# Attention over 1,601 keys: a smaller first piece ahead of the loop, swapped keys read across quadrants, key parts written by ScalarE

## The chip, the cores and the metric

The kernel runs on one core of one Trainium2 chip. The metric is device time in microseconds of one execution. Three runs of the kernel before gave 707.81, 712.16 and 712.87 us; the median is 712.16 us. The execution that was profiled took 710.4 us, of which 707.4 us lie between its first and last instruction.

## What is computed

`x` has 4 batches of 256 rows of 128, `ctx_1024` 4 batches of 1,601 rows of 128. All is float32, with 16 heads of 8.

```python
x = x + L0_xattn(layernorm(x), ctx)       # layernorm again on both sides, rotary turn of q and k, a bias by distance, gate
x = x + tanh(layernorm(x) @ W1 @ W2 @ W3 + b)
x = x + L1_xattn(layernorm(x), ctx, ctx)  # plain projections with biases, mask, softmax, output projection
x = x + experts(layernorm(x))             # two of 8 experts by a gate
```

The rotary turn of layer 0 is `k * cos + swapped(k) * sin`, where `swapped` exchanges the halves of each head. Scores must be exact to float32, so a key or query is stored as three bfloat16 parts (high, middle, low) whose products are summed in one matmul.

## The kernel before

The context is cut into 13 tiles of 124 keys, and four groups of 4 heads go over each tile. That gives 52 units per batch and layer, and 416 in all: units 0 to 207 are layer 0 (batches 0 to 3), the others layer 1. TensorE (PE) runs one written-out loop over pairs of units: `scores` of the next two units (matmuls L369 for the bias, L375 for q times k), then `beside` (side work by a table of slots), then `values` of this pair (L390), then `beside` again. A slot is the number of the unit within its batch. ScalarE (ACT) turns each unit's scores into `probs` by one Exp (L811). PSUM banks 0 to 3 hold scores, 4 and 5 the sums, and two side banks, LOW (6) and HIGH (7), all side work. A side bank is filled again only when what was in it has been read (`seen`).

The keys and values of layer 0 are made chunk by chunk, as side work of the batch before: `keys_at` gives the slots. `CHUNKS` is 4, 3, 3 and 3 tiles. For each chunk PE makes the turned and the swapped key product (L314, two banks, with weights `w0c[:, 2]` and `w0c[:, 3]`), the layer 1 key product (L317) and the values (L323). VectorE (DVE) multiplies by the tables (L950, L955), adds the two (L959), casts high parts (L965, L976) and middle parts (L1000, L1002), adds the layer 1 bias (L974) and writes the values (L992, L994). GpSimd (POOL) makes the rests and the low parts (L740 to L746). SyncE (SP) issues the DMAs that place six copies of the parts in `k_side` (L609) and store them for layer 1 (L610 to L616).

SP works its list strictly in the order written, and a wait holds all behind it. At the start it loads all of `x`, all tokens of batch 0 (L582, L583) and then the weights (L661); ACT's list loads the tables, the constant rows of `k_side` and `q_side` and the bias. Ahead of the loop come the norm and the queries of all of `x`, and chunk 0 of batch 0. A small sample of scores then gives each row's shift (`sample`, `make_shift` L1028, DMA L648), on which the scores of unit 0 wait. The same shift gates every batch: `scores` of a batch's unit 0 waits for `shift_in`. A batch's row scales go from `turn_rstd` (L305) through DRAM (L594, L600) to `norm_context` on POOL (L730), which the batch's chunk 0 needs.

The mask is checked in 16 pieces, loaded from POOL's queue (L723) and reduced on DVE (L1014), all beside layer 0.

## Time and profile before

| | |
|---|---|
| median of three runs | 712.16 us |
| profiled execution | 710.4 us, span 707.4 us |
| PE busy | 576.8 us (82%) |
| ACT busy | 408.8 us (58%) |
| DVE busy | 269.7 us (38%) |
| POOL busy | 119.3 us (17%) |
| first Exp of the loop | at 89.3 us |
| batches 0 to 3 of layer 0 (first Exp to first Exp) | 114.2, 88.7, 79.7, 61.8 us |
| batches 0 to 3 of layer 1 | 55.6, 60.7, 59.2, 57.0 us |
| from the last unit to the end | about 41 us |

Busy shares are means over stages that have different limits. So the stages are read one by one: which engine works all the time, and what ends the waits of PE and ACT.

### The profile page before, as it was taken

What the parts mean: (1) busy time and instruction counts of PE and PEld (TensorE: products, weight loads), DVE (VectorE), ACT (ScalarE), POOL (GpSimd) and SP (SyncE); (2) the same over time, 40 slices, a digit from 0 to 9 for tenths busy, and PEclk for the clock granted to TensorE, in tenths of its full rate; (3) what the DMA queues carried; (4) which work ended last, traced back from release to release, by engine and by line L of the source; (5) the groups of instructions that cost most, each with busy time, mean ns of one, the idle gap of its engine ahead of it and who ended that gap; (6) DMA issues with size and microseconds to landing.
All of it is one profiled execution on the core that took longest, in us unless ns stands there. A gap on an engine that the chain in (4) does not pass through costs nothing.

```text
span 707.4 us, 15097 instructions
## 1 busy us (share of the span) xinstructions
PE 576.8 (82%) x6349; PEld 284.5 (40%) x6349; DVE 269.7 (38%) x703; ACT 408.8 (58%) x437; POOL 119.3 (17%) x132
## 2 busy tenths in 40 slices
PE   4046199589759889989999999999989998999744
PEld 2033045335334445544554544443443443353231
DVE  0036246246615662266525112320540443243243
ACT  1001055336435465754777789899859878988600
POOL 1043123343414340054200100000000000000000
PEclk9998579789969999999999999999999999999955
DMA  9542417749472766017718103602700720000000
GB/s 234 119 143 68 130 33 196 223 120 247 127 231 70 178 167 224 23 38 192 204 56 184 63 3 68 151 2 48 171 9 1 158 66 5 2 2 9 2 0 11
DMA packets 55496, 70.37 MB, mean 99 GB/s; under 512 B 5684, under 2 KB 47680, under 8 KB 55360
## 3 DMA queue, kind: packets, MB, share of 16 engines
q1 hardware_dynamic: 52576, 57.82, 30.7%
q0 software_dynamic: 1280, 6.56, 3.9%
q10 hardware_dynamic: 1568, 4.99, 3.0%
q8 instruction: 51, 0.84, 0.5%
q14 instruction: 21, 0.17, 0.1%
HBM read 37.45 MB, written 18.84 MB: 80 GB/s over the span
## 4 chain that ended last, share of the span: by engine, by line
PE 58%; issue 11%; DVE 9%; DMA 8%; ACT 7%; SPq 3%; POOL 2%; POOLq 0%; ACTq 0%; DVEq 0%
PE ps L390 20%; PE ps L375 11%; PE ps L369 7%; ACT probs L811 6%; DMA ctx_tokens<-in_ctx 5%; PE ps L323 4%; PE ps L314 3%; PE ps L317 2%; PE ps L503 2%; SPq L609 1%; DVE y L1194 1%; PE ps L437 1%; DMA r_scratch<-rstd_turned 1%; PE ps L424 1%; PE ps L430 1%
## 5 line engine op out<-in xcount | busy, mean ns | idle before, releaser
L811 ACT ACTIVATE probs<-ps 124x1024 f32<-124x1024 f32 (+1 forms) x416 | 399.8, 1022 | 200.2 <-PE ps L375 198.1
L390 PE MATMUL ps<-probs,values 124*9 124x256 f32 (+1 forms) x3328 | 223.3, 387 | 0.4 <-DVE out_sums L1035 0.4
L375 PE MATMUL ps<-q_side,k_side 63*124 63x256 bf16 (+1 forms) x1664 | 164.2, 283 | 11.6 <-ACT probs L811 9.8
L375 PEld LDWEIGHTS ps<-q_side,k_side 63*124 63x124 bf16 (+1 forms) x1664 | 98.6, 133 | 86.1 <-ACT probs L811 55.6
L390 PEld LDWEIGHTS ps<-probs,values 124*9 124x9 f32 (+1 forms) x3328 | 71.3, 90 | 100.2 <-issue 43.5
L369 PE MATMUL ps<-bias_g,bias_w 64*124 64x512 bf16 (+1 forms) x416 | 87.2, 415 | 14.7 <-DMA q_side<-shift 14.1
L753 POOL TENSOR_TENSOR post_rstd<-post_rstd,power 128x2 f32<-128x2 f32 x12 | 8.4, 697 | 319.6 <-DVE post_rstd L1083 319.6
L369 PEld LDWEIGHTS ps<-bias_g,bias_w 64*124 64x124 bf16 (+1 forms) x416 | 28.2, 132 | 56.8 <-issue 36.9
L1035 DVE COPY out_sums<-ps 128x512 f32<-128x512 f32 x16 | 11.0, 690 | 94.2 <-PE ps L390 94.2
L314 PE MATMUL ps<-ctx_normed,w_centred 128*128 128x372 f32 (+2 forms) x64 | 28.5, 572 | 7.1 <-POOL ctx_normed L730 6.6
L1021 DVE TENSOR_REDUCE sample_max<-ps 128x8 f32<-128x512 f32 x32 | 20.6, 686 | 32.2 <-PE ps L340 32.2
L323 PE MATMUL ps<-w_values,ctx_turned 128*124 128x256 f32 (+1 forms) x104 | 32.1, 426 | 0.0
L1194 DVE SCALAR_TENSOR_TENSOR y<-ps,comb,y 128x128 f32<-128x128 f32 x64 | 22.5, 351 | 15.8 <-PE ps L503 13.9
L740 POOL TENSOR_TENSOR k<-k,k_parts 128x372 f32<-128x372 f32 (+2 forms) x16 | 15.0, 937 | 71.7 <-DVE k_parts L965 71.7
L317 PE MATMUL ps<-ctx_turned,wk_sb 128*128 128x372 f32 (+2 forms) x32 | 16.6, 604 | 10.2 <-DVE k L950 10.2
L845 ACT ACTIVATE w_centred<-ps 128x512 f32<-128x512 f32 x1 | 0.6, 597 | 41.8 <-PE ps L267 41.8
L261 PE MATMUL ps<-gamma_beta,w 128*128 128x1 f32 x8 | 1.9, 354 | 26.3 <-DMA wvg_sb<-in_wvg 26.3
L992 DVE TENSOR_TENSOR values<-ps,rstd 124x256 f32<-124x256 f32 (+2 forms) x32 | 12.0, 375 | 29.2 <-PE ps L323 29.2
L323 PEld LDWEIGHTS ps<-w_values,ctx_turned 128*124 128x124 f32 (+1 forms) x104 | 18.1, 196 | 12.1 <-issue 10.0
L744 POOL TENSOR_TENSOR k_parts<-k,k_parts 128x372 bf16<-128x372 f32 (+2 forms) x16 | 16.0, 1001 | 39.5 <-DVE k_parts L1000 39.5
L925 DVE BATCH_NORM_STATS2 row_stats<-ctx_tokens 124x6 f32<-124x128 f32 (+1 forms) x52 | 11.3, 279 | 29.0 <-DMA ctx_tokens<-in_ctx 29.0
L950 DVE SCALAR_TENSOR_TENSOR k<-ps,beta_products,k_cos_sb 128x372 f32<-128x372 f32 (+2 forms) x16 | 10.1, 633 | 26.7 <-PE ps L314 26.5
(177 smaller groups left out, 485.9 us busy)
## 6 DMA issues: line engine op xcount, KB each, us to landing
k_side<-k_scratch SPq DMA_DIRECT2D x24, 400.2 KB, 8.8
k_side<-k_parts SPq DMA_DIRECT2D x48, 93.0 KB, 3.9
k_scratch<-k_parts SPq DMA_DIRECT2D x16, 279.0 KB, 4.2
v_scratch<-values SPq DMA_DIRECT2D x4, 936.0 KB, 6.2
values<-v_scratch SPq DMA_DIRECT2D x4, 936.0 KB, 14.1
mask_q<-in_mask POOLq DMA_DIRECT2D x8, 400.5 KB, 5.0
ctx_turned<-in_ctx_t SPq DMA_DIRECT2D x4, 800.5 KB, 7.0
ctx_normed<-r_scratch SPq DMA_DIRECT2D x4, 800.5 KB, 4.1
```

The source lines that it names most:

```text
L314: pe.matmul(ps[:, bank, 0:w], w0c[:, i, :], cn[:, k_0:k_1], start=True, stop=True).then_inc(made[bank], 1)
L317: pe.matmul(ps[:, LOW, 0:w], wk1[:], ct[:, k_0:k_1], start=True, stop=True).then_inc(made[LOW], 1)
L323: last = pe.matmul(ps[0:r, bank, 2 * D * i:2 * D * i + 2 * D], ct[:, TS * t:TS * t + r], wvv[:].rearrange("p l d -> p (l d)"), start=True, ...
L369: pe.matmul(ps[0:width, bank, :], G["bias_w"][rows, at], G["bias_g"][rows, t:t + 1, :].broadcast_to((HALF, 2, SQ)), start=True, stop=False ...
L375: last = pe.matmul(ps[0:width, bank, SQ * i:SQ * (i + 1)], kst[rows, j % 2, 2 * g + i, at], qst[rows, j % 2, 2 * g + i, :], start=not bias ...
L390: last = pe.matmul(ps[32 * i:32 * i + VC, ACC + g // 2, SQ * (g % 2):SQ * (g % 2) + SQ], v[0:rows, j % 2, t, h, :], p[0:rows, u % 4, SQ * ...
L503: pe.matmul(ps[:, bank, :], xn[:, b * SQ + 128 * t:b * SQ + 128 * t + 128], ew[:, 4 * i:4 * i + 4, :].rearrange("p e d -> p (e d)"), start ...
L740: pool.tensor_tensor(ka[:, s, 0:w], ka[:, s, 0:w], kp0[:, s, 0, 0:w], ALU.subtract).then_inc(rest0, 1)
L744: pool.tensor_tensor(kp0[:, s, 2, 0:w], ka[:, s, 0:w], kp0[:, s, 1, 0:w], ALU.subtract).then_inc(lo0, 1)
L811: act.activation(p[0:rows, u % 4, :], ps[0:rows, s:s + 2, :].rearrange("p a n -> p (a n)"), ACT.Exp)\
L1021: dve.tensor_reduce(mx[:, c, H8 * half_:H8 * half_ + H8], ps[:, bank, :].rearrange("p (h k) -> p h k", k=SAMPLE), AX.X, ALU.max).then_inc( ...
L1194: add = dve.scalar_tensor_tensor(out=out[:, t, :], in0=ps[:, bank, D * i:D * i + D], scalar=comb[:, t, e:e + 1], in1=out[:, t, :], op0=ALU ...
```

## The change

The chunks become 1, 4, 4 and 4 tiles. Only the first 256 rows of `x` are normed and projected ahead of the loop, and chunks 0 and 1 (5 tiles) of batch 0; the other queries, and the centred `x`, are made in slots 11, 13, 17 and 19 of batch 0. The row statistics of `x` come from a second copy of it with rows on the partitions (`x_tok`), by the same instructions as those of the tokens. The row scales of batch 0 are spread by matmuls (L290 of the kernel after) and no longer go through DRAM. SP's order of loads is new and now also carries the tables, the constant rows and the bias; ACT's list carries the weights. `store_keys` is split in `place_keys` and `store_keys`.

The swapped key product is gone: DVE reads the one product in four pieces of 32 partitions, each from 32 partitions away, against a sine table that is rearranged. The sum of the two goes to POOL, the layer 1 bias and all high and middle parts to ACT, 3 to 9 units after the matmul. The mask check moves to the batches from 3 on (batch 3 of layer 0, and 0 to 2 of layer 1).

SP's queue from the tokens of batch 1 to the shift of batch 0, first before and then after the change (`lo0` counts low parts written, `q_lo` those of the queries, `bn_done` token statistics, `side6_read` readings of LOW):

```order
L582 DMA ctx_tokens<-in_ctx 124x12x128 [waits bn_done]
L583 DMA ctx_tokens<-in_ctx 113x128
L627 DMA q_side<-q_parts 16x8x256 [waits q_lo]
L627 DMA q_side<-q_parts 16x8x256 x5
L609 DMA k_side<-k_parts 16x8x496 [waits lo0]
L609 DMA k_side<-k_parts 16x8x496 x5
L610 DMA k_scratch<-k_parts 384x1x496
L612 DMA v_scratch<-v 128x576 [waits side6_read]
L614 DMA k_scratch<-k_parts 384x1x496 [waits lo1]
L648 DMA q_side<-shift 1x8x256 [waits side6_read]
L648 DMA q_side<-shift 1x8x256
```

```order
L646 DMA k_side<-k_parts 16x8x124 [waits lo0]
L646 DMA k_side<-k_parts 16x8x124 x5
L669 DMA q_side<-q_parts 16x8x256 [waits q_lo]
L669 DMA q_side<-q_parts 16x8x256 x5
L646 DMA k_side<-k_parts 16x8x496 [waits lo0]
L646 DMA k_side<-k_parts 16x8x496 x5
L614 DMA ctx_tokens<-in_ctx 124x128 [waits bn_done]
L614 DMA ctx_tokens<-in_ctx 124x4x128 [waits bn_done] x2
L614 DMA ctx_tokens<-in_ctx 124x3x128 [waits bn_done]
L617 DMA ctx_tokens<-in_ctx 113x128
L690 DMA q_side<-shift 1x8x256 [waits side6_read,gaps_in0]
L690 DMA q_side<-shift 1x8x256
```

The tokens of batch 1 were ahead of the queries and the keys and now stand between the keys and the shift; the stores of keys and values now follow the shift.

DVE's work on one chunk of keys (chunk 1 of batch 1), before and after (`side6_filled` and `side7_filled` count fillings of LOW and HIGH):

```order
L950 SCALAR_TENSOR_TENSOR k<-ps,beta_products,k_cos_sb 128x372 [waits side6_filled,lo0]
L955 SCALAR_TENSOR_TENSOR k_swapped<-ps,beta_products,k_sin_sb 128x372 [waits k0_full,side7_filled]
L959 TENSOR_TENSOR k<-k,k_swapped 128x372 [waits side7_read,side6_read]
L965 CAST k_parts<-k 128x372 [waits k0_full,k0_out1,k_in3]
L974 TENSOR_SCALAR k<-ps,columns_sb 128x372 [waits side6_filled,k1_out1,lo1]
L976 CAST k_parts<-k 128x372 [waits side6_read]
L992 TENSOR_TENSOR values<-ps,rstd 124x32x8 [waits side7_filled,v1_out1]
L994 COPY v<-ps 124x32x8
L992 TENSOR_TENSOR values<-ps,rstd 124x16x8 [waits side6_filled]
L994 COPY v<-ps 124x16x8
L1000 CAST k_parts<-k 128x372 [waits rest0]
L1002 CAST k_parts<-k 128x372 [waits rest1]
```

```order
L1119 SCALAR_TENSOR_TENSOR k<-ps,beta_products,k_cos_sb 128x496 [waits side6_filled,lo0,table_in0]
L1126 SCALAR_TENSOR_TENSOR k_swapped<-ps,beta_products,k_sin_sb 32x496 [waits k0_full]
L1126 SCALAR_TENSOR_TENSOR k_swapped<-ps,beta_products,k_sin_sb 32x496 x3
L1153 TENSOR_TENSOR values<-ps,rstd 124x32x8 [waits side6_filled,v1_out1]
L1155 COPY v<-ps 124x32x8
L1153 TENSOR_TENSOR values<-ps,rstd 124x32x8 [waits side7_filled]
L1155 COPY v<-ps 124x32x8
```

Twelve instructions for 3 tiles became nine for 4; all five table products read LOW, which stays taken until the last.

ACT's list behind the first units of batch 0 held Exps alone until the gate of batch 1; now it reads:

```order
L889 ACTIVATE probs<-ps 124x1024 [waits scores_ready] x4
L915 ACTIVATE k<-ps,columns_sb 128x496 [waits side7_filled,k1_out0,lo1]
L916 ACTIVATE k_parts<-ps,columns_sb 128x496
L889 ACTIVATE probs<-ps 124x1024 [waits probs_used,scores_ready] x3
L932 ACTIVATE k_parts<-k 128x496 [waits k0_full,k0_out0,k_in0]
L889 ACTIVATE probs<-ps 124x1024 [waits probs_used,scores_ready]
L922 ACTIVATE k_parts<-k 128x496 [waits rest1]
L889 ACTIVATE probs<-ps 124x1024 [waits probs_used,scores_ready] x2
L938 ACTIVATE k_parts<-k 128x496 [waits rest0]
```

Five key instructions per chunk stand between the Exps, three of them behind POOL (`k0_full`, `rest1`, `rest0`).

The diff, cut to its core:

```diff
-CHUNKS = [(0, 4), (4, 7), (7, 10), (10, KT)]
+CHUNKS = [(0, 1), (1, 5), (5, 9), (9, KT)]
...
+KEY_STEPS = [1 + (t1 - t0 + 1) // 2 for t0, t1 in CHUNKS]
...
-        first = {0: (0, 1), 6: (0, 2), 12: (0, 3), 23: (1, 0), 29: (1, 1), 36: (1, 2), 43: (1, 3)}
+        first = {0: (0, 2), 6: (0, 3), 23: (1, 0), 26: (1, 1), 33: (1, 2), 40: (1, 3)}
     elif j < NB - 1:
-        first = {6 + 6 * n: (j + 1, n) for n in range(NC)}
+        first = {at: (j + 1, n) for n, at in enumerate((6, 9, 16, 23))}
     else:
         return None
     for at, (b, n) in first.items():
-        if slot - at in (0, 2, 3, 4):
-            return b, n, (0, 2, 3, 4).index(slot - at)
+        if slot - at in (0, 2, 3)[:KEY_STEPS[n]]:
+            return b, n, (0, 2, 3).index(slot - at)
...
-                    for bank, i in ((LOW, 2), (HIGH, 3)):
-                        fill(bank, "k0", b, n)
-                        pe.matmul(ps[:, bank, 0:w], w0c[:, i, :], cn[:, k_0:k_1], start=True, stop=True).then_inc(made[bank], 1)
-                elif k == 1:
-                    fill(LOW, "k1", b, n)
-                    pe.matmul(ps[:, LOW, 0:w], wk1[:], ct[:, k_0:k_1], start=True, stop=True).then_inc(made[LOW], 1)
+                    fill(LOW, "k0", b, n)
+                    pe.matmul(ps[:, LOW, 0:w], w0c[:, 2, :], cn[:, k_0:k_1], start=True, stop=True).then_inc(made[LOW], 1)
+                    fill(HIGH, "k1", b, n)
+                    pe.matmul(ps[:, HIGH, 0:w], wk1[:], ct[:, k_0:k_1], start=True, stop=True).then_inc(made[HIGH], 1)
                 else:
-                    bank, tiles = ((HIGH, range(t0, t0 + 2)), (LOW, range(t0 + 2, t1)))[k - 2]
+                    bank, tiles = (LOW, HIGH)[k - 1], range(t0 + 2 * (k - 1), min(t0 + 2 * k, t1))
                     fill(bank, "v", b, n)
...
-            x_means()
-            x_variances()
             beta_products()
+            centre_weights()
             pe.wait_ge(ident_in, 16)
-            turn_rstd(0)
-            pe.wait_ge(both_pow, 1)
-            for last in spread_x(rb, (4, 5)):
-                last.then_inc(spread, 1)
-            centre_weights()
-            pe.wait_ge(seen[LOW], side.of(LOW, "weights"))
+            pe.wait_ge(rs_ready, 1)
+            spread_rstd(4, 0).then_inc(r_spread, 1)
+            pe.wait_ge(x_pow, 1)
+            spread_x(3, 0, range(2), 1).then_inc(spread, 1)
             first_queries()
-            pe.wait_ge(seen[HIGH], side.of(HIGH, "weights"))
-            pe.wait_ge(cols_in, 48)
-            for k in range(4):
+            pe.wait_ge(wk1_in, 32)
+            for k in range(KEY_STEPS[0]):
                 keys(0, 0, k)
-            pe.wait_ge(gaps_in, 64)
+            pe.wait_ge(rs_ready, 2)
+            spread_rstd(5, 1).then_inc(r_spread, 1)
+            for k in range(KEY_STEPS[1]):
+                keys(0, 1, k)
+            pe.wait_ge(gaps_in[0], 64)
             for c in range(2):
                 sample(0, c)
             turn_maxima(0)
+            pe.wait_ge(rs_ready, 3)
+            for n, bank in ((2, LOW), (3, HIGH)):
+                fill(bank, "r", n)
+                spread_rstd(bank, n).then_inc(made[bank], 1)
+            pe.wait_ge(x_pow, 2)
+            pe.wait_ge(cn_ready, 2)
+            spread_x(4, 0, range(2, 6), 1).then_inc(spread, 1)
+            spread_x(5, 0, range(6, XT), 1).then_inc(spread, 1)
+            pe.wait_ge(const_in, 48)
+            pe.wait_ge(qa_scaled, 2)
+            for u in range(2):
+                scores(u)
             pe.wait_ge(zeroed, 1)
+            pe.wait_ge(xq_ready, 2)
...
+            load_tokens(0, 0)
+            sp.dma_start(xtok[:, 0:2, :], G["x_tok"][:, 0:2, :]).then_inc(xtok_in, 16)
+            load_tokens(0, 1)
+            sp.dma_start(x[:, 0:SQ], G["x_t"][:, 0:SQ]).then_inc(x_in, 16)
+            load_turned_chunk(0, 0)
+            load_turned_chunk(0, 1)
+            load_tables(0)
+            load_tokens(0, 2)
+            load_tokens(0, 3)
+            sp.dma_start(xtok[:, 2:XT, :], G["x_tok"][:, 2:XT, :]).then_inc(xtok_rest_in, 16)
+            sp.dma_start(x[:, SQ:NT], G["x_t"][:, SQ:NT]).then_inc(xrest_in, 16)
+            for n in (2, 3):
...
+            load_tables(1)
+            for r in (HD - 2, HD - 1):
+                sp.dma_start(kst[r::HD, 0].rearrange("p h k -> p (h k)"), G["ones_row"].broadcast_to((H, H8 * SKP))).then_inc(gaps_in[0], 16)
+                sp.dma_start(qst[r::HD].rearrange("p s h n -> p (s h n)"), G["zero_row"].broadcast_to((H, 2 * H8 * SQ))).then_inc(gaps_in[0], 16)
+            for dst, src in ((G["bias_w"], "bias_k"), (G["bias_g"], "bias_q"), (G["pick"], "pick_in")):
+                sp.dma_start(dst[:], G[src]).then_inc(const_in, 16)
+            place_keys(0, 0)
             load_queries_of(0)
+            place_keys(0, 1)
+            for n in range(NC):
+                load_tokens(1, n)
+            sp.wait_ge(gaps_in[0], 64)
+            load_shift(0)
             store_keys(0, 0)
-            load_shift(0)
+            store_keys(0, 1)
+            for r in (HD - 2, HD - 1):
+                sp.dma_start(kst[r::HD, 1].rearrange("p h k -> p (h k)"), G["ones_row"].broadcast_to((H, H8 * SKP))).then_inc(gaps_in[1], 16)
+            for n in (2, 3):
+                place_keys(0, n)
+                store_keys(0, n)
             for n in late:
                 if n != "columns":
                     sp.dma_start(late[n][:], G[n]).then_inc(late_in, 16)
-            for n in range(1, NC):
-                store_keys(0, n)
             load_turned(1)
...
+                pool.wait_ge(seen[HIGH], side.of(HIGH, "k1", b, n))
+                pool.tensor_tensor(k1[:, s, 0:w], k1[:, s, 0:w], kp1[:, s, 0, 0:w], ALU.subtract).then_inc(rest1, 1)
+                pool.wait_ge(seen[LOW], side.of(LOW, "k0", b, n))
+                pool.tensor_tensor(ka[:, s, 0:w], ka[:, s, 0:w], kb[:, 0:w], ALU.add).then_inc(k0_full, 1)
                 pool.wait_ge(hi0, c + 1)
                 pool.tensor_tensor(ka[:, s, 0:w], ka[:, s, 0:w], kp0[:, s, 0, 0:w], ALU.subtract).then_inc(rest0, 1)
-                pool.wait_ge(hi1, c + 1)
-                pool.tensor_tensor(k1[:, s, 0:w], k1[:, s, 0:w], kp1[:, s, 0, 0:w], ALU.subtract).then_inc(rest1, 1)
+                pool.wait_ge(mid1, c + 1)
+                pool.tensor_tensor(kp1[:, s, 2, 0:w], k1[:, s, 0:w], kp1[:, s, 1, 0:w], ALU.subtract).then_inc(lo1, 1)
                 pool.wait_ge(mid0, c + 1)
                 pool.tensor_tensor(kp0[:, s, 2, 0:w], ka[:, s, 0:w], kp0[:, s, 1, 0:w], ALU.subtract).then_inc(lo0, 1)
-                pool.wait_ge(mid1, c + 1)
-                pool.tensor_tensor(kp1[:, s, 2, 0:w], k1[:, s, 0:w], kp1[:, s, 1, 0:w], ALU.subtract).then_inc(lo1, 1)
...
+            for j in range(NB - 1, NJ - 1):
+                first = 4 * (j - NB + 1)
+                look_at_mask(first)
+                look_at_mask(first + 1)
+                if j <= NB:
+                    for k in range(2):
+                        post_power(2 * (j - 1) + k)
+                    look_at_mask(first + 2)
+                    query_parts(j - 1)
+                else:
+                    post_power(2 * NB + j - NB - 1)
+                    look_at_mask(first + 2)
+                look_at_mask(first + 3)
+            post_power(3 * NB - 2)
+            post_power(3 * NB - 1)
...
+                for lag, part in ((9, middle_of_first), (7, middle_of_second), (6, high_of_first), (3, second_keys)):
+                    key = keys_at(j, i - lag)
+                    if key is not None and key[2] == 0:
+                        part(*key[:2])
...
-                dve.wait_ge(made[HIGH], side.of(HIGH, "k0", b, n))
+                                         op0=ALU.add, op1=ALU.mult)
                 if c:
                     dve.wait_ge(k0_full, c)
-                dve.scalar_tensor_tensor(out=kb[:, 0:w], in0=ps[:, HIGH, 0:w], scalar=beta_cols[:, 3:4], in1=k_sin[:, k_0:k_1],
-                                         op0=ALU.add, op1=ALU.mult).then_inc(seen[HIGH], 1)
-                dve.wait_ge(seen[LOW], side.of(LOW, "k0", b, n))
-                dve.wait_ge(seen[HIGH], side.of(HIGH, "k0", b, n))
-                dve.tensor_tensor(ka[:, s, 0:w], ka[:, s, 0:w], kb[:, 0:w], ALU.add).then_inc(k0_full, 1)
-                if c >= 2:
-                    b2, n2 = chunk_before(b, n, 2)
-                    dve.wait_ge(k_in[n2], QL * (b2 + 1))
-                    dve.wait_ge(k0_out[s], 16 * (c // 2))
-                dve.wait_ge(k0_full, c + 1)
-                dve.tensor_copy(kp0[:, s, 0, 0:w], ka[:, s, 0:w]).then_inc(hi0, 1)
-
-            def second_keys(b, n):
-                c, s = NC * b + n, n % 2
-                w = CHUNK_KEYS[n][1] - CHUNK_KEYS[n][0]
-                if c >= 2:
-                    dve.wait_ge(lo1, c - 1)
-                    dve.wait_ge(k1_out[s], 16 * (c // 2))
-                dve.wait_ge(made[LOW], side.of(LOW, "k1", b, n))
-                dve.tensor_scalar(k1[:, s, 0:w], ps[:, LOW, 0:w], col["bk"], None, ALU.add).then_inc(seen[LOW], 1)
-                dve.wait_ge(seen[LOW], side.of(LOW, "k1", b, n))
-                dve.tensor_copy(kp1[:, s, 0, 0:w], k1[:, s, 0:w]).then_inc(hi1, 1)
-
-            def both_values(b, n):
+
+                for to in range(0, 128, 32):
+                    at = to ^ 32
+                    last = dve.scalar_tensor_tensor(out=kb[to:to + 32, 0:w], in0=ps[at:at + 32, LOW, 0:w], scalar=beta_cols[at:at + 32, 2:3],
+                                                    in1=k_sin[at:at + 32, k_0:k_1], op0=ALU.add, op1=ALU.mult)
+                last.then_inc(seen[LOW], 1)
```

## Rows read from the trace of the kernel before

**Rows 1.** The page, the chain that ended last, by engine
```profile
PE 58%; issue 11%; DVE 9%; DMA 8%; ACT 7%; SPq 3%; POOL 2%; POOLq 0%; ACTq 0%; DVEq 0%
```

**Rows 2.** Busy us by stage: PE, PEld, DVE, ACT, POOL; then clock, DMA share, GB/s
```profile
0.00:38.00 38.00, 7.33 (x20) 4.67 (x20) 1.57 (x4) 2.43 (x3) 2.90 (x7) 1.00 0.74 177
89.30:203.50 114.20, 90.69 (x851) 45.67 (x849) 52.14 (x149) 50.41 (x52) 40.93 (x42) 0.86 0.60 172
203.50:292.20 88.70, 83.23 (x873) 42.70 (x871) 44.38 (x118) 51.13 (x54) 25.26 (x27) 0.95 0.50 140
292.20:372.00 79.80, 77.09 (x860) 39.56 (x858) 39.62 (x84) 51.15 (x55) 24.01 (x28) 1.00 0.42 113
305.00:345.00 40.00, 37.87 (x370) 19.10 (x364) 26.57 (x57) 21.32 (x22) 15.84 (x19) 1.00 0.56 146
```

**Rows 3.** Timeline of the start: start us, us, engine, line; idle before
```profile
1.64 30.94 SPq L583 DMA_DIRECT2D ctx_tokens<-in_ctx  x1
...
72.28 3.83 SPq L609 DMA_DIRECT2D k_side<-k_parts  x6
...
80.27 0.61 PE L340 MATMUL ps<-k_side,q_side 62*128 62x64 bf16 x16 [10.44 <-DMA k_side<-k_parts]
...
88.16 0.69 PE L369 MATMUL ps<-bias_g,bias_w 64*124 64x512 bf16 x2 [2.40 <-DMA q_side<-shift]
```

**Rows 4.** DMA packets in 53 to 62 us and in 124 to 139 us
```profile
DMA packets 1208, 0.62 MB, mean 69 GB/s; under 512 B 0, under 2 KB 1208, under 8 KB 1208
...
DMA packets 2204, 3.55 MB, mean 237 GB/s; under 512 B 218, under 2 KB 1882, under 8 KB 2202
```

**Rows 5.** Timeline, hand-over of row scales to batch 1
```profile
124.13 3.81 SPq L609 DMA_DIRECT2D k_side<-k_parts  x6
...
129.24 0.38 PE L305 MATMUL ps<-ident,rstd 124*13 124x124 f32 x1 [4.91 <-POOL rstd L734]
...
144.88 3.46 PE L314 MATMUL ps<-ctx_normed,w_centred 128*128 128x496 f32 x4 [6.07 <-POOL ctx_normed L730]
```

**Rows 6.** Timeline, hand-over of the shift to batch 1
```profile
190.15 3.83 SPq L609 DMA_DIRECT2D k_side<-k_parts  x6
...
202.40 0.69 PE L369 MATMUL ps<-bias_g,bias_w 64*124 64x512 bf16 x2 [11.73 <-DMA q_side<-shift]
```

**Rows 7.** Groups of the page: count, busy us, mean ns, idle before
```profile
L314 PE MATMUL ps<-ctx_normed,w_centred 128*128 128x372 f32 (+2 forms) x64 | 28.5, 572 | 7.1 <-POOL ctx_normed L730 6.6
```

**Rows 8.** The same by shape
```profile
L744 POOL TENSOR_TENSOR k_parts<-k,k_parts 128x496 bf16<-128x496 f32 x4 | 4.9, 1232 | 10.3 <-DVE k_parts L1000 10.3
...
L955 DVE SCALAR_TENSOR_TENSOR k_swapped<-ps,beta_products,k_sin_sb 128x496 f32<-128x496 f32 x4 | 2.9, 731 | 0.7 <-PE ps L314 0.6
...
L1014 DVE TENSOR_REDUCE checks<-mask_q 128x1 f32<-128x801 int32 x8 | 7.7, 968 | 0.0
...
L1028 DVE TENSOR_SCALAR shift<-ps 16x256 bf16<-16x256 f32 x8 | 3.3, 411 | 11.5 <-PE ps L350 11.5
...
L297 PE MATMUL ps<-out_sums,w_centred 128*128 128x512 f32 x8 | 3.7, 605 | 0.5 <-ACT w_centred L845 0.5
...
L851 ACT ACTIVATE q_parts<-att 128x512 bf16<-128x512 f32 x2 | 1.2, 622 | 4.3 <-DVE att L903 4.3
```

**Rows 9.** Timeline inside batch 2, PE and DVE
```profile
307.37 1.05 PE L390 MATMUL ps<-probs,values 124*9 124x256 f32 x16
...
308.35 1.13 PE L323 MATMUL ps<-w_values,ctx_turned 128*124 128x256 f32 x4
...
309.41 0.43 PE L369 MATMUL ps<-bias_g,bias_w 64*124 64x512 bf16 x2
...
310.43 1.13 PE L323 MATMUL ps<-w_values,ctx_turned 128*124 128x256 f32 x4
...
313.81 0.33 DVE L1044 TENSOR_SCALAR inside<-den 128x256 bf16<-128x256 f32 x1
...
318.48 0.60 DVE L950 SCALAR_TENSOR_TENSOR k<-ps,beta_products,k_cos_sb 128x372 f32<-128x372 f32 x1
...
318.99 0.60 DVE L955 SCALAR_TENSOR_TENSOR k_swapped<-ps,beta_products,k_sin_sb 128x372 f32<-128x372 f32 x1
...
319.13 0.89 PE L317 MATMUL ps<-ctx_turned,wk_sb 128*128 128x372 f32 x2 [2.13 <-DVE k L950]
```

**Rows 10.** Who waited for whom, PE: us in total, times, longest us
```profile
PE ps L305 <- POOL rstd L734: 10.8, 3, 4.9
```

675 lines of the change are left out of this document (395 added, 280 removed).

## The prediction

> **What bounds the kernel now.** I read the chain that ended last first: PE holds 58% of it [rows 1], so a stage counts by what PE waits for in it. The table by stage comes next [rows 2]. In the first 38 us PE is busy for 7.3 us and the DMA engines for 74%: this stage is bound by transfers. In batch 0 PE is busy 90.7 of 114.2 us, in batch 1 83.2 of 88.7, in batch 2 77.1 of 79.8, while ACT, with its 52 Exps, is busy about 51 us in each: layer 0 is bound by PE, plus PE's waits. In the timeline of the start the reader should see one issue on SP's queue that takes 30.9 us (the tokens of 512 B rows, beside ACT's large loads), keys placed from 72.3 us, the sample at 80.3 and the first scores at 88.2 [rows 3]. Last come two hand-overs where PE stands still: 4.9 and 6.1 us for the row scales [rows 5], 11.7 us for the shift [rows 6].
>
> **The start: -22.7 us.** The work ahead of the loop shrinks to 5 tiles and 256 rows, so arithmetic no longer sets its end; SP's queue does. Ahead of the first keys it now carries 1,601 token rows and 1,024 rows of `x`, 2,625 packets of 512 B, and 5.4 MB in larger ones; ACT's queue adds 0.9 MB. Packets of 512 B ran at 1,208 in 9 us, 134 per us [rows 4]: 20 us. The other 6.2 MB take 26 us at the 237 GB/s of a busy stretch [rows 4]. One after the other that is 46 us; wholly overlapped at 237 GB/s, 7.6 MB take 32. I take 40, starting at 1 us. Keys of chunk 0, queries and keys of chunk 1 follow: 3 + 5.7 (768 packets of 512 B) + 3.8 (as an issue of six, [rows 3]) = 12.5 us, to 53.5. The sample needs only the first two; from the sample to the first scores it was 88.2 - 80.3 = 7.9 us [rows 3], so by itself the shift could be there at about 57. But the tokens of batch 1 now stand between: 1,601 packets, 12 us. The shift lands at 65.5, and the first scores move from 88.2 to 65.5. Bounds: at the 177 GB/s of the first 38 us [rows 2], 9.7 MB take 55 us and with the tail the scores start at 80 (-8); if the large loads hide the small packets, at 52 (-36). What is late next is the shift, behind those tokens.
>
> **PE's work inside the loop: -9 us.** The turned and swapped products were 64 passes, 28.5 us [rows 7]; 60 lie inside the loop, half go: -13.3. One tile fewer of the other products: -0.8 (values of two tiles take 1.06 us, 308.35 to 309.41, [rows 9]). Added are the late queries and the centred `x`: a 512-column product takes 3.7 / 4 = 0.93 us [rows 8], five of these: +4.7. All of it is on the path.
>
> **LOW is held longer: +9.6 us.** DVE frees LOW after five instructions of 496 columns. One took 731 ns, and pieces of 32 partitions should cost no less: 16 partitions by 256 take 411 ns [rows 8], and nothing in the rows makes fewer partitions cheaper. DVE begins one before the last ends: 318.48 to 318.99 for one that lasts 0.60 [rows 9], so 4 x 0.66 + 0.73 = 3.4 us, 3.6 with both ends. PE wants LOW again after the layer 1 product (0.95), values (0.98, 307.37 to 308.35), scores (1.02, 309.41 to 310.43) [rows 9], near 3.0: it waits 0.6 us in nine chunks, +5.4. In batches 1 and 2 the second chunk comes three slots after the first, with the softmax finish (4.7 us, 313.81 to 318.48, [rows 9]) between them on DVE. PE waited 2.13 us there before [rows 9]. Now: finish 4.7 + table products 3.4, less the some 4 us that PE takes to come round, is 4.2; twice 2.1 more, +4.2. Below, if the pieces overlap better and finish fits: 0. Above: double, 19.
>
> **ACT's new work: 0 us.** 11 chunks x 5 instructions x 0.6 us (a 512-column one takes 622 ns, [rows 8]) = 33 us, 3 for the small chunks, 2 for queries: 38. The cover is ACT's idle time beside PE: in 40 us of batch 2 it was busy 21.3 [rows 2] and gets about 15 more. The writes fall 3, 6, 7 and 9 units after a chunk's product, mostly beside the next side work. If the cover were gone, all 38 would show.
>
> **POOL's sum, DVE's relief, no DRAM trip for batch 0's scales: 0.** POOL has 5 instructions of 1.1 to 1.23 us [rows 8] per chunk, 6 us in the 11 that a chunk's seven slots last; it was busy 25 of 89 us.
>
> **Hand-overs.** The scales of batch 1 now wait on POOL until the last parts of batch 0 are made (ACT writes a middle part after unit 15), then on SP behind the placing, the stores and 0.5 MB of late weights. Before, from the last placing at 124.1 to the first product it was 20.8 us [rows 5]; the mask load is gone (-0.4 MB), the late weights come (+4 us), PE arrives 8 slots and two centring steps later. I get 3 + 6.5 us of waiting against 4.9 + 6.1 before: 0, bounds -4 and +7. The shift of batch 1 took 12.2 us from the placing at 190.2 [rows 6]; now one more tile and the load of the next context (0.8 MB) are ahead, the mask is not: **+2** (0 to +8). Of the 10.8 us for the power [rows 10] the third wait goes, since POOL makes it one chunk earlier: **-2.7**.
>
> **The mask beside layer 1: +3.** 16 reductions of 0.97 us [rows 8] leave DVE beside batches 0 to 2, where DVE rarely ended PE's waits, and join a chain that PE follows closely; batch 3 had one there already. I take 1 us in each of three batches (0 to +12).
>
> **Sum:** -22.7 - 9 + 9.6 + 0 + 2 - 2.7 + 3 = -19.8, from the profiled 710.4 to 690.6. The median lies 1.8 above the profiled execution: **692 us**.
>
> **The rivals.**
> - *No overlap between the pieces.* The four change quadrant each time. If DVE starts each after the last has ended, it is 5 x 0.73 + 5 x 0.04 = 3.85 us, +0.45 in 11 chunks: **697 us**. For it: only instructions on the same partitions are seen overlapping [rows 9]. The Trainium skill, "VectorE: DVE Perf Modes", section "Two Vector instructions with no wait between them", has such a rule: an instruction whose input or output starts in another quadrant than the last one in that memory starts only when all earlier ones have finished. No run here shows such a piece; by that rule this rival is the forecast.
> - *A late queue.* The loads run at the pace of the first 38 us, and the tokens hold the shift until 78: start -10, **705 us**. For it: one issue was held for 30.9 us [rows 3].
> - *Nothing is late.* Start at 55 and half of LOW's waits: -10 - 5, **677 us**. Against it: the 12 us of tokens are plain in the order.
> - *ScalarE's line (slower).* ACT works in order, and three of five key writes wait for POOL, which waits for DVE. If POOL is late, the Exps behind stand, and PE's next scores with them, in each of 11 chunks. It decides from 20 of the 38 us on: then the gain is gone (**712**); with all, **730 us**. For it: after the finish in batches 1 and 2 DVE is late by 4 us. Against: ACT has 19 free us in 40 [rows 2].
>
> **How the numbers follow.** Forecast (684 to 696) 0.42; no overlap (694 to 702) 0.22; nothing late (675 to 684) 0.14; late queue (702 to 709) 0.11; ScalarE's line (709 to 730) 0.07; a hand-over that grows by more, anywhere, 0.04. The range 677 to 707 leaves out under 0.2. The three runs span 5 us, so about 1% is what a measurement tells from no change: faster means under 705. That is 0.42 + 0.22 + 0.14 + 0.05 = 0.83; within 1% 0.09; slower 0.08.
>
> **What would show it.** First Exp at 66 to 67 us, the DMA engines busy without a gap before it, and PE's wait there ended by the shift. In batches 1 and 2 PE waits for a DVE table product, 0.6 us a chunk and 4 at the second. Starts of the four pieces 0.65 us apart (or 0.75 and more: no overlap). ACT's idle time ended by scores, not by POOL; if `k0_full` or `rest0` ends many of its waits, the forecast is wrong on the slow side. The wait for the shift of batch 1 is 12 to 15 us. If the first Exp comes before 58 or after 74, the queue was misjudged.

## The result: 1.6% slower, and the profile after

The changed kernel took 721.47 us (median of four runs, 720.17 to 723.66) against 710.84 us before (four runs, 707.81 to 712.87). The ratio is 1.0156, with a 95% interval from 1.0105 to 1.0208. The forecast was 692 us with a range of 677 to 707: wrong in sign. The profiled execution took 723.66 us, its span is 721.9.

First Exp to first Exp of each batch, from the two timelines, in us:

| | start | 0 | 1 | 2 | 3 | 4 | 5 | 6 | 7 |
|---|---|---|---|---|---|---|---|---|---|
| before | 89.3 | 114.2 | 88.7 | 79.7 | 61.8 | 55.6 | 60.7 | 59.2 | 57.0 |
| after | 59.6 | 122.9 | 90.5 | 85.7 | 72.5 | 55.6 | 68.7 | 68.4 | 57.0 |
| difference | -29.7 | +8.7 | +1.8 | +6.0 | +10.7 | 0 | +8.0 | +9.2 | 0 |

The start gained even more than forecast. The loop of layer 0 gave 16.5 us of it back, and batches 3, 5 and 6, in which the only new work is the check of the mask, gave back 27.9. Batch 4 carries four pieces of the mask as well and did not change.

The page of the kernel after, the chain that ended last, by engine and by line (against [rows 1]):

```profile
PE 50%; DVE 13%; issue 12%; ACT 8%; DMA 8%; SPq 6%; POOL 2%; POOLq 0%; DVEq 0%; ACTq 0%
PE ps L411 18%; PE ps L395 9%; ACT probs L889 7%; PE ps L389 7%; DVE k_swapped L1126 5%; DMA mask_q<-in_mask 4%; PE ps L341 4%; PE ps L333 2%; DVE y L1348 2%; SPq L646 2%; PE ps L524 1%; DMA ctx_tokens<-in_ctx 1%; DVE k L1119 1%; DMA q_side<-shift 1%; DVE den L1203 1%
```

PE's share fell from 58 to 50% and DVE's rose from 9 to 13. Two names are new on the chain, the four pieces of the swapped product (5%) and three loads of the mask (4%; 10.8, 10.2 and 10.1 us, in batches 3, 5 and 6).

Busy us by stage of the kernel after, columns as in [rows 2]: the start and batches 0, 1, 2, 3 and 5.

```profile
0.00:38.00 38.00, 17.92 (x46) 12.07 (x46) 17.75 (x68) 6.98 (x14) 13.13 (x21) 0.87 0.75 203
59.60:182.50 122.90, 89.61 (x845) 44.76 (x843) 48.33 (x128) 65.83 (x84) 41.66 (x37) 0.87 0.48 146
182.50:273.00 90.50, 82.29 (x864) 43.23 (x863) 38.00 (x102) 59.87 (x75) 26.83 (x27) 0.92 0.39 119
273.00:358.70 85.70, 78.38 (x850) 40.14 (x848) 32.66 (x68) 59.87 (x75) 25.71 (x28) 0.94 0.28 86
358.70:431.10 72.40, 64.36 (x804) 32.06 (x800) 19.23 (x38) 51.10 (x54) 7.01 (x11) 0.93 0.35 89
486.80:555.50 68.70, 60.53 (x709) 27.07 (x710) 24.50 (x61) 49.68 (x54) 2.92 (x5) 0.90 0.33 83
```

In batch 2 PE has less to do than before and is busy longer, 78.38 us against 77.09 [rows 2]: its granted clock is 0.94 where it was 1.00. Batches 3 and 5, at 0.93 and 0.90 here, looked like this before, in the same columns:

```profile
372.00:433.80 61.80, 61.15 (x806) 30.76 (x802) 16.02 (x35) 51.20 (x54) 4.08 (x6) 1.00 0.31 71
...
489.50:550.10 60.60, 55.83 (x708) 25.31 (x708) 20.84 (x57) 49.61 (x53) 0.70 (x1) 0.97 0.30 67
```

The start, timeline of SP's queue and of PE (against [rows 3]):

```profile
26.39 3.85 SPq L646 DMA_DIRECT2D k_side<-k_parts  x6
...
42.85 6.07 SPq L614 DMA_DIRECT2D ctx_tokens<-in_ctx  x4
48.95 2.45 SPq L617 DMA_DIRECT2D ctx_tokens<-in_ctx  x1
51.52 3.50 SPq L690 DMA_DIRECT2D q_side<-shift  x2
```
```profile
58.46 0.69 PE L389 MATMUL ps<-bias_g,bias_w 64*124 64x512 bf16 x2 [3.75 <-DMA q_side<-shift]
```

The keys are placed from 26.4 us where it was 72.3, and the order of the queue is the one that the prediction read: tokens of batch 1, then the shift.

What PE waited for in the kernel after (us in total, times, longest):

```profile
PE ps L341 <- DVE k_swapped L1126: 21.8, 12, 3.8
PE ps L389 <- DMA q_side<-shift: 18.2, 2, 14.5
PE ps L395 <- ACT probs L889: 16.5, 35, 3.7
PE ps L389 <- ACT probs L889: 11.5, 13, 3.7
...
PE ps L445 <- DVE x L1255: 8.1, 2, 7.8
...
PE ps L333 <- POOL ctx_normed L796: 5.8, 1, 5.8
...
PE ps L325 <- POOL rstd L801: 1.8, 1, 1.8
```

**Batch 3, the mask.** Timelines of POOL, DVE and PE (the number in brackets is idle time before, and what ended it):

```profile
367.64 0.75 POOL L790 DMA_DIRECT2D mask_q<-in_mask  x1
```
```profile
370.73 0.42 DVE L1211 TENSOR_REDUCE checks<-inside 128x1 f32<-128x256 bf16 x1
378.45 0.99 DVE L1168 TENSOR_REDUCE checks<-mask_q 128x1 f32<-128x801 int32 x1 [7.31 <-DMA mask_q<-in_mask]
379.36 0.47 DVE L1247 TENSOR_SCALAR post<-ps,folded_bias 128x256 f32<-128x256 f32 x1
```
```profile
381.27 1.22 PE L445 MATMUL ps<-x,ones_mean 128*128 128x256 f32 x2 [7.78 <-DVE x L1255]
```

POOL issues the first mask load at 367.6, after the query parts. The load lands 10.8 us later. DVE, in order, stands at the reduction for 7.31 us with the gate of batch 2 (L1247 to L1255) behind it, and PE stands 7.78 us at the mean that needs the gate. In batch 5 it is the second piece, loaded into the same buffer only after the first is reduced, ahead of the choice of experts. This load took 10.2 us:

```profile
498.54 0.55 POOL L790 DMA_DIRECT2D mask_q<-in_mask  x1 [26.16 <-DVE checks L1168]
```
```profile
508.77 0.99 DVE L1168 TENSOR_REDUCE checks<-mask_q 128x1 f32<-128x800 int32 x1 [4.16 <-DMA mask_q<-in_mask]
509.68 0.17 DVE L1296 TENSOR_TENSOR gate_scores<-ps,gate_b_sb 128x16 f32<-128x16 f32 x1
...
510.29 0.17 DVE L1303 TENSOR_TENSOR gate_scores<-gate_scores,gate_top 128x16 f32<-128x16 f32 x1
```
```profile
510.50 0.22 ACT L904 ACTIVATE gate_p<-gate_scores 128x16 f32<-128x16 f32 x1 [4.00 <-DVE gate_scores L1303]
510.62 3.75 ACT L889 ACTIVATE probs<-ps 124x1024 f32<-124x1024 f32 x4
```
```profile
511.68 0.69 PE L395 MATMUL ps<-q_side,k_side 63*124 63x256 bf16 x4 [3.71 <-ACT probs L889]
```

The wait is handed on twice: DVE's 4.16 us become ACT's 4.00, because the gate's small Exp stands in ACT's line with four large ones behind it, and ACT's become PE's 3.71.

**Batch 1, the second chunk**, the slot at which PE waited 2.13 us in batch 2 before [rows 9]. DVE, then PE, then two windows (columns as in [rows 2]):

```profile
202.00 1.75 DVE L1203 RECIPROCAL den<-den 128x256 f32<-128x256 f32 x1
...
205.78 2.97 DVE L1126 SCALAR_TENSOR_TENSOR k_swapped<-ps,beta_products,k_sin_sb 32x496 f32<-32x496 f32 x4
```
```profile
208.80 2.07 PE L341 MATMUL ps<-w_centred,ctx_turned 128*124 128x256 f32 x4 [3.28 <-DVE k_swapped L1126]
```
```profile
199.00:205.00 6.00, 6.00 (x62) 2.96 (x62) 4.73 (x11) 3.26 (x5) 0.82 (x2) 1.00 0.28 74
208.80:215.00 6.20, 6.20 (x32) 3.71 (x36) 1.11 (x4) 2.13 (x3) 0.84 (x2) 0.55 0.01 3
```

PE waits 3.28 us. In the 6 us that hold the work before it the granted clock is 1.00, the level of 2.4 GHz; in the 6.2 us behind it 0.55, so nearly all at 1.2 GHz. The same four score products show it, before and behind the wait:

```profile
203.71 0.38 PE L395 MATMUL ps<-q_side,k_side 63*124 63x256 bf16 x4
...
211.27 0.63 PE L395 MATMUL ps<-q_side,k_side 63*124 63x256 bf16 x4
```

PE was busy for all of the 6.2 us; at the full clock the same work would have taken about 3.4 (an estimate, 6.2 x 0.55), so this wait costs nearly its own length once more. In the kernel before, the 2.13 us wait of batch 2 cost nothing more, for the clock stayed at 1.00 [rows 2]; behind the 2.42 us wait of batch 1 it was 0.72 for 6.2 us.

### The profile page after: what moved, and what is told of

Read it like the earlier page. It is cut to its first block, busy times and chain, and to the rows that moved or that the text cites. A ratio compares the mean times of both kernels' runs of the same rounds, so it can differ in the third digit from the quotient of the medians.

```text
span 721.9 us, 15140 instructions
## 1 busy us (share of the span) xinstructions
PE 585.5 (81%) x6326; PEld 290.2 (40%) x6326; DVE 266.7 (37%) x682; ACT 443.0 (61%) x514; POOL 132.0 (18%) x146
## 4 chain that ended last, share of the span: by engine, by line
PE 50%; DVE 13%; issue 12%; ACT 8%; DMA 8%; SPq 6%; POOL 2%; POOLq 0%; DVEq 0%; ACTq 0%
PE ps L411 18%; PE ps L395 9%; ACT probs L889 7%; PE ps L389 7%; DVE k_swapped L1126 5%; DMA mask_q<-in_mask 4%; PE ps L341 4%; PE ps L333 2%; DVE y L1348 2%; SPq L646 2%; PE ps L524 1%; DMA ctx_tokens<-in_ctx 1%; DVE k L1119 1%; DMA q_side<-shift 1%; DVE den L1203 1%
## 5 line engine op out<-in xcount | busy, mean ns | idle before, releaser
L395 PE MATMUL ps<-q_side,k_side 63*124 63x256 bf16 (+1 forms) x1664 | 169.0, 290 | 18.3 <-ACT probs L889 16.5
L389 PE MATMUL ps<-bias_g,bias_w 64*124 64x512 bf16 (+1 forms) x416 | 89.7, 427 | 30.0 <-DMA q_side<-shift 18.2
L389 PEld LDWEIGHTS ps<-bias_g,bias_w 64*124 64x124 bf16 (+1 forms) x416 | 28.7, 134 | 74.4 <-issue 36.8
L341 PE MATMUL ps<-w_centred,ctx_turned 128*124 128x256 f32 (+1 forms) x104 | 35.2, 468 | 21.8 <-DVE k_swapped L1126 21.8
L1189 DVE COPY out_sums<-ps 128x512 f32<-128x512 f32 x16 | 11.0, 690 | 90.6 <-PE ps L411 90.6
L790 POOL DMA_DIRECT2D mask_q<-in_mask x16 | 9.1, 567 | 186.1 <-DVE checks L1168 186.1
L1126 DVE SCALAR_TENSOR_TENSOR k_swapped<-ps,beta_products,k_sin_sb 32x496 f32<-32x496 f32 (+2 forms) x64 | 40.4, 632 | 0.9
L341 PEld LDWEIGHTS ps<-w_centred,ctx_turned 128*124 128x124 f32 (+1 forms) x104 | 20.2, 217 | 34.2 <-DVE k_swapped L1126 27.5
L1119 DVE SCALAR_TENSOR_TENSOR k<-ps,beta_products,k_cos_sb 128x496 f32<-128x496 f32 (+2 forms) x16 | 10.1, 633 | 54.7 <-PE ps L333 54.7
L812 POOL TENSOR_TENSOR k<-k,k_parts 128x496 f32<-128x496 f32 (+2 forms) x16 | 15.1, 944 | 49.6 <-ACT k_parts L916 49.6
L333 PE MATMUL ps<-ctx_normed,w_centred 128*128 128x496 f32 (+2 forms) x32 | 17.9, 648 | 6.7 <-POOL ctx_normed L796 5.8
L816 POOL TENSOR_TENSOR k<-k,k_parts 128x496 f32<-128x496 f32 (+2 forms) x16 | 15.1, 943 | 42.4 <-ACT k_parts L932 42.4
L1168 DVE TENSOR_REDUCE checks<-mask_q 128x1 f32<-128x801 int32 (+1 forms) x16 | 15.6, 978 | 19.0 <-DMA mask_q<-in_mask 18.9
L524 PE MATMUL ps<-expert_w_sb,xn 128*128 128x512 f32 x32 | 20.2, 758 | 1.1 <-DVE y L1341 0.6
```

Source lines behind the costliest of these rows:

```text
L333: pe.matmul(ps[:, LOW, 0:w], w0c[:, 2, :], cn[:, k_0:k_1], start=True, stop=True).then_inc(made[LOW], 1)
L341: last = pe.matmul(ps[0:r, bank, 2 * D * i:2 * D * i + 2 * D], ct[:, TS * t:TS * t + r], wvv.rearrange("p l d -> p (l d)"), start=True, st ...
L389: pe.matmul(ps[0:width, bank, :], G["bias_w"][rows, at], G["bias_g"][rows, t:t + 1, :].broadcast_to((HALF, 2, SQ)), start=True, stop=False ...
L395: last = pe.matmul(ps[0:width, bank, SQ * i:SQ * (i + 1)], kst[rows, j % 2, 2 * g + i, at], qst[rows, j % 2, 2 * g + i, :], start=not bias ...
L524: pe.matmul(ps[:, bank, :], xn[:, b * SQ + 128 * t:b * SQ + 128 * t + 128], ew[:, 4 * i:4 * i + 4, :].rearrange("p e d -> p (e d)"), start ...
L1119: dve.scalar_tensor_tensor(out=ka[:, s, 0:w], in0=ps[:, LOW, 0:w], scalar=beta_cols[:, 2:3], in1=k_cos[:, k_0:k_1], op0=ALU.add, op1=ALU.mult)
```

## The experiments

Each row of the table gives the median of an experiment and its stages. "Changed" is the kernel of this case at 721.47 us; ratios are to runs of the kernel before on the same chip. Those had medians from 709.4 to 713.5 us, and a stage that no edit touches differs by up to 2 us between two profiles (batch 1: 90.5, 88.8, 88.8 and 90.7 in the first four rows). So a difference of 2 or 3 us between two rows is not read as an effect, unless both stood on one chip, as "both that paid" and "and the shift ahead" did.

| kernel | us | ratio, 95% interval | start | 0 | 1 | 2 | 3 | 5 | 6 |
|---|---|---|---|---|---|---|---|---|---|
| changed | 721.5 | 1.016 [1.011, 1.021] | 59.6 | 122.9 | 90.5 | 85.7 | 72.5 | 68.7 | 68.4 |
| no mask | 693.8 | 0.979 [0.977, 0.982] | 59.5 | 122.9 | 88.8 | 83.9 | 61.4 | 60.7 | 60.7 |
| reductions only | 694.5 | 0.979 [0.975, 0.984] | 58.7 | 123.1 | 88.8 | 83.9 | 61.8 | 60.7 | 60.7 |
| mask late | 696.4 | 0.979 [0.972, 0.985] | 59.6 | 122.2 | 90.7 | 85.2 | 61.4 | 60.7 | 60.7 |
| mask back | 709.7 | 0.997 [0.994, 1.000] | 60.1 | 132.9 | 89.8 | 86.6 | 61.8 | 59.2 | 59.2 |
| before, mask moved | 727.5 | 1.028 [1.022, 1.034] | 87.7 | 109.8 | 84.8 | 79.7 | 74.1 | 68.9 | 65.0 |
| one piece | 707.7 | 0.996 [0.993, 0.999] | 59.9 | 117.4 | 84.6 | 81.1 | 72.2 | 68.9 | 68.4 |
| same quadrant (no mask) | 688.0 | 0.966 [0.960, 0.972] | 58.0 | 123.2 | 89.4 | 83.9 | 61.4 | 60.7 | 59.2 |
| later second | 709.5 | 0.996 [0.993, 0.999] | 59.3 | 123.7 | 82.3 | 79.1 | 73.7 | 69.4 | 68.7 |
| later parts | 722.8 | 1.015 [1.008, 1.021] | 60.0 | 124.1 | 89.4 | 85.6 | 70.1 | 69.5 | 68.5 |
| short parts | 716.7 | 1.005 [1.002, 1.009] | | | | | | | |
| shift first | 722.9 | 1.019 [1.014, 1.023] | 55.0 | 126.4 | 90.6 | 85.2 | 72.6 | 69.1 | 68.2 |
| both that paid | 682.6 | 0.962 [0.959, 0.966] | 59.9 | 121.7 | 84.6 | 79.1 | 61.4 | 59.2 | 60.7 |
| and the shift ahead | 680.0 | 0.959 [0.955, 0.962] | 59.8 | 119.5 | 84.4 | 79.1 | 61.4 | 59.2 | 60.7 |
| and batch 0's slots | 678.6 | 0.952 [0.948, 0.956] | 59.7 | 118.9 | 85.5 | 79.1 | 61.4 | 59.2 | 59.2 |

### Is it the mask?

**Mask back.** POOL issues a piece after a chunk's parts, DVE reduces it after the next chunk's keys:

```diff
                 for n in range(NC):
                     parts(b, n)
+                    look_at_mask(4 * b + n)
...
                 keys(j + 1, 0)
+                look_at_mask(4 * j + 3)
                 finish(j - 1)
                 keys(j + 1, 1)
+                look_at_mask(4 * j + 4)
```

> The changed kernel with the mask loads and their reductions put back beside layer 0 (as before the change: POOL issues a piece after each chunk's parts, DVE reduces it after the next chunk's keys); nothing else differs. Theory A, the place of the mask is what failed: batches 3, 5 and 6 give back 10.7 + 8.0 + 9.2 = 27.9 us (72.5, 68.7 and 68.4 us become about 62, 61 and 59), and layer 0 pays at most 5 us for the reductions: 721.5 - 28 + 3 = 696 us (692 to 702). Rival B, the later batches are slower for another reason (the clock that PE was granted, or buffers that come free later): batches 3, 5 and 6 stay within 3 us of 72, 69 and 68, and the time stays above 714.

Batches 3, 5 and 6 came back as theory A says, to 61.8, 59.2 and 59.2. But the time was 709.7 and not 696, for batch 0 became 10 us longer: I had put three early pieces in the hand-over to batch 1, where DVE now stood three times (12.7 us in all) for a mask load ahead of the keys of that batch. It looks like the same mechanism in another place, brought in by my edit; no run isolates it.

**No mask.** `look_at_mask` is not called on either engine, and `dve.memset(checks[:, 2 * NB:6 * NB], 1.0)` stands in for its results.

> The changed kernel without the mask's pieces: neither their 16 loads nor the 16 reductions, with the 16 check values set to 1 instead, so this leaves a part of the computation out. Theory A: batches 3, 5 and 6 as in the kernel before (62, 61, 59), layer 0 as in the changed kernel: 721.5 - 28 = 693.5 us, and 0 to 5 us below the kernel with the mask back beside layer 0; that difference is what the check costs in its old place. Rival B: above 714.

693.8: theory A to within 1 us. The mask costs the changed kernel 27.7 us (26 by the two ratios). Between the two profiled executions batches 3, 5 and 6 differ by 26.8 us; batches 1 and 2 differ by 3.5, though neither kernel looks at the mask there. The sums of PE and the others over batches 3, 5 and 6, the changed kernel first:

```profile
sum 209.50, PE 185.27 PEld 86.19 DVE 68.19 ACT 150.42 POOL 12.29; mean PE 61.76 PEld 28.73 DVE 22.73 ACT 50.14 POOL 4.10
```
```profile
sum 182.80, PE 172.87 PEld 81.54 DVE 57.42 ACT 150.42 POOL 5.48; mean PE 57.62 PEld 27.18 DVE 19.14 ACT 50.14 POOL 1.83
```

PE has the same work in both. Of the 26.7 us, 14.1 are waits (23.1 against 9.0 us in these batches) and 12.4 are PE's own busy time, at a granted clock of 0.93, 0.90 and 0.90 where it is 1.00, 0.97 and 0.97 without the mask.

**Before, mask moved.** The same move alone, in the kernel before.

> The kernel before, with the mask's loads and reductions moved beside layer 1 to exactly the places that the change gave them, and nothing else. Theory A, this move alone costs what it costs in the changed kernel: batches 3, 5 and 6 become 11, 8 and 8 us longer (about 72, 68 and 68), layer 0 gets 2 us or less back, and the time is 711 + 26 = 737 us (730 to 741). Rival B, the cost needs the rest of the change (POOL's later queue, the transfers from the earlier start): batch 3 is longer by 4 us or less, and the time stays under 727.

Batches 3, 5 and 6 grew by 12.3, 8.2 and 5.8 us, 26.3 in all, so the rest of the change is not needed for it. The total rose by 18 (727.5 against 709.4 us on the same chip), which is below theory A's 730: batches 0 and 1 gave 4.4 and 3.9 us back, where 2 were expected. So in its old place the check was not free either, as far as one profile of each shows.

### Reductions, loads, or their order?

**Reductions only.** The 16 reductions stand where the change put them; POOL's `look_at_mask` is `pass`, and the buffer is filled with 1.

> The changed kernel with the 16 reductions of the mask in their places on VectorE, but no loads: the buffer is filled with 1 at the start, so the check of the mask is left out. Theory A1, what VectorE waits for is the load (7.3 us in batch 3, 4.2 us in batches 5 and 6): without it batch 3 falls from 72.5 to 65 or less, batches 5 and 6 from 68.5 to 62 or less, and the time is 700 us or less. Theory A2, the 0.97 us of each reduction ahead of the gate, the choice and the sample are enough to bring PE to waits and a lower clock: half of the 28 us or more stay, 708 or more.

694.5, the time without any mask: theory A1. At the same place of batch 5 DVE does not stop:

```profile
489.38 0.42 DVE L1238 TENSOR_TENSOR xn<-xn,ps 128x256 f32<-128x256 f32 x1 [2.04 <-PE ps L458]
489.72 0.98 DVE L1164 TENSOR_REDUCE checks<-mask_q 128x1 f32<-128x800 int32 x1
490.61 0.17 DVE L1292 TENSOR_TENSOR gate_scores<-ps,gate_b_sb 128x16 f32<-128x16 f32 x1
```

The 15.6 us of reductions, the only price that the prediction gave them, are worth nothing. The whole cost comes with the loads: PE's waits that they lead to, and its slower clock behind those.

**Mask late.** Same 16 loads, same 16 reductions; each stands behind what PE needs:

```diff
-                if j < NJ - 1:
+                if j == NB:
                     look_at_mask(first)
                 if j <= NB:
                     gate(j - 1)
-                    look_at_mask(first + 1)
+                    if j == NB:
+                        look_at_mask(first + 1)
                     second_queries(j - 1)
                     query_parts(j - 1)
+                    if j < NB:
+                        look_at_mask(first)
                 else:
                     project(j - NB - 1)
                     if j < NJ - 1:
-                        look_at_mask(first + 1)
+                        look_at_mask(first)
                     choose(j - NB - 1)
-                    weigh(j - NB - 1)
+                    weigh(j - NB - 1, first + 1 if j < NJ - 1 else None)
...
                     make_shift(j + 1)
-                    look_at_mask(first + 3)
+                    for i in range(1 if j < NB else 3 if j == NB else 2, 4):
+                        look_at_mask(first + i)
```

> The changed kernel with the same 16 mask loads and 16 reductions beside layer 1, but none of them ahead of work that PE waits for: in batch 3 the first reduction stands behind the query parts and the other three behind the shift; in batches 5 to 7 the first stands behind the projection, the second in the weighing, the last two behind the shift. Theory A, the cost of 30 us (721.5 against 693.8 without the mask) is the order on VectorE, the reductions and their loads standing ahead of the gate, of the choice of experts and of the sample: batches 3, 5 and 6 come down to 62 to 63, 60 to 61 and 60 to 61 us, and the time is 695 (693 to 699). Rival B, it is the load on the DMA queues and on memory (the loads are there as before): less than half of it comes back, 707 or more.

(`weigh` reduces the piece behind its first copy; POOL's loads follow the same order.) 696.4, theory A. DVE still waits for mask loads, 16.5 us in 5 waits (first row) against 18.9 in 5 in the changed kernel (second):

```profile
DVE checks L1175 <- DMA mask_q<-in_mask: 16.5, 5, 3.7
```
```profile
DVE checks L1168 <- DMA mask_q<-in_mask: 18.9, 5, 7.3
```

Nearly the same waits, 25 us apart: what counts is what stands behind them. The loads were no faster (3.2 to 12.0 us from issue to landing, 3.3 to 10.8 in the changed kernel). After the shift of the next batch DVE has nothing to do until the sums are copied: in the changed kernel it stood idle for 15 us there. The 2.6 us that are left against no mask are within the noise.

### The four pieces

**One piece.** One instruction of 128 partitions, `kb[:, 0:w]` from `ps[:, LOW, 0:w]`, in place of the four.

> The changed kernel with the swapped product as one instruction of 128 partitions in place of the four that read 32 partitions away; the halves are then not swapped, so the keys of layer 0 are other ones. Theory A, the four pieces in a row (2.96 us by the trace, 0.74 each) hold the LOW bank: PE's waits for the table product (21.8 us in 12) go to under 5, and the batches 0 to 2 give back 12 to 18 us: about 706. Rival B, LOW is not what PE lacks: PE then waits for the next thing (Exps held by ScalarE's key writes, POOL's sum), and the time falls by less than 6 us, to 716 or more.

707.7, theory A: batches 0 to 2 gave 5.5, 5.9 and 4.6 us. PE's waits for the table product in batches 1 and 2 fell from 9.8 to 2.0. So three extra pieces in each of 14 chunks of the loop cost 14 us by the medians, 16 by the stages. In batches 1 and 2 only a part of that is waits: those for Exps rose from 5.6 to 8.0 us, and PE's busy time fell from 160.7 to 155.5.

**Same quadrant.** `kb[0:32, i]` from `ps[0:32, LOW]` four times.

> The kernel without the mask's pieces (as the one measured at 693.8 us) in which the four pieces of the swapped product all read the first 32 partitions and write the first 32 partitions of four buffers; the sum takes the first of them. The keys of layer 0 are other ones, and the mask is left out. Theory A, the pieces of the changed kernel start 0.74 us apart because each reads and writes other partitions than the one ahead: on the same 32 partitions they start 0.65 or less apart, the four take 2.6 us or less, and the time falls by 3 to 5 us. Rival B, four instructions of 496 columns that read PSUM take that long anyway (the length is in the columns): 2.9 to 3.0 us again, and the time stays within 2 us of 693.8.

The same four instructions, first on the same partitions, then as the change has them (both without the mask):

```profile
28.45 0.73 DVE L1112 SCALAR_TENSOR_TENSOR k<-ps,beta_products,k_cos_sb 128x496 f32<-128x496 f32 x1
29.10 2.64 DVE L1118 SCALAR_TENSOR_TENSOR k_swapped<-ps,beta_products,k_sin_sb 32x496 f32<-32x496 f32 x4
```
```profile
29.22 0.73 DVE L1113 SCALAR_TENSOR_TENSOR k<-ps,beta_products,k_cos_sb 128x496 f32<-128x496 f32 x1
29.97 2.96 DVE L1120 SCALAR_TENSOR_TENSOR k_swapped<-ps,beta_products,k_sin_sb 32x496 f32<-32x496 f32 x4
```

They start 0.64 us apart on the same 32 partitions and 0.74 to 0.76 where each reads and writes others; the first starts 0.65 behind the table product in one and 0.75 in the other. So the rival "no overlap" holds, and with it the rule of the Trainium skill, "VectorE: DVE Perf Modes", section "Two Vector instructions with no wait between them". It is worth 0.4 us a chunk. PE's waits for table products fell from 21.7 to 16.3 us, but the medians differ by 5.8 us and the two profiled spans by 2.3, so the price in time is not settled.

### The second chunk's slot, and ScalarE

**Later second.**

```diff
-        first = {at: (j + 1, n) for n, at in enumerate((6, 9, 16, 23))}
+        first = {at: (j + 1, n) for n, at in enumerate((6, 11, 18, 25))}
```

> The changed kernel with the chunks of batches 2 and 3 at the slots 6, 11, 18, 25 in place of 6, 9, 16, 23. Theory A, the second chunk's product finds VectorE in the softmax finish: PE's waits for the table product of up to 3.8 us in batches 1 and 2 go, 3 us each, and the Exp's waits with them: 5 to 8 us less, 715. Rival B, the parts are only made later, the sample of the next batch meets them, and the time stays within 2 us of 721.5.

709.5, 12 us less and more than theory A gave: batches 1 and 2 lost 8.2 and 6.6 us in the profile.

```profile
183.00:265.30 82.30, 77.06 (x864) 40.39 (x862) 38.06 (x102) 59.88 (x74) 26.87 (x27) 0.99 0.43 131
265.30:344.40 79.10, 74.18 (x850) 38.34 (x848) 32.67 (x68) 59.89 (x74) 25.77 (x28) 1.00 0.31 93
```

PE's waits for table products and Exps there went from 15.4 to 9.7 us, 5.7 less. The other 9.4 of the 15 are PE's own busy time, 77.06 and 74.18 against 82.29 and 78.38, with the clock at 0.99 and 1.00 in place of 0.92 and 0.94. Batches 0 and 3 were some 1 us longer each. On top of mask late the same slots gave 6.1 us in each of batches 1 and 2, 13.8 by the medians.

**Later parts.** The lags of ScalarE's writes, in units after the product: `((10, middle_of_first), (8, high_of_first), (7, middle_of_second), (3, second_keys))`, from 9, 6, 7 and 3.

> The changed kernel with ScalarE writing the high part of the first layer's keys 8 units after the chunk's product in place of 6, and the middle part 10 after in place of 9. Theory A, the 11.5 us that PE's scores wait for the Exp (13 times, up to 3.7) come from ScalarE standing at the high part for POOL's sum (15.1 us, 5 times): these waits fall under 5 us and 7 us come back, 714.5. Rival B, the parts are then late for the buffers of the chunk after next (the product three slots later), and the wait moves to VectorE and to the LOW bank: within 2 us of 721.5.

722.8, rival B in the number. ScalarE's waits for POOL's sum fell from 15.1 to 6.5 us, and PE's for the Exps went from 11.5 to 11.0. ScalarE came to wait elsewhere, 5.2 us for a store of the parts and 4.8 for another result of POOL, 16.5 us in all as in the changed kernel. The edit only moved its waits, so it does not show what they cost.

**Short parts.** In three of the five writes `w = 32 if b else w`.

> The changed kernel in which, from batch 1's chunks on, three of ScalarE's five key writes (the high and the middle part of the first layer's keys, the middle part of the second's) write 32 columns in place of up to 496; the rest of these parts is left out, so the keys are other ones. It takes some 12 x 3 x 0.35 = 13 us of ScalarE's work away and leaves every wait in its order. Theory A, ScalarE's occupation by these writes holds the Exps (PE waits 11.5 us for them in layer 0): the waits fall to 5 us or less, and 6 to 12 us come back, 710 to 715. Rival B, ScalarE stands in order behind POOL's sum, and the length of the writes is covered as the prediction had it: the waits stay at 9 us or more, and the time within 3 us of 721.5.

716.7, 4.8 us less, or 7 by the two ratios: between the theories by the one, theory A by the other. Its profiled execution took 6.4 us more than its median, so its stages are left out, and which wait shrank stays open; in that execution PE still waited 9.3 us for the Exps at L389. ScalarE's busy time fell by 10.3 us, from 443.0 to 432.7. So the writes are not wholly covered as the prediction had it; the runs do not tell whether half of their length shows, or more.

### SP's order

**Shift first.** In SP's list `load_shift(0)` stands before the four `load_tokens(1, n)`.

> The changed kernel with one move on SP's queue: the shift of batch 0 is sent before the four token loads of batch 1 instead of behind them. By the step of the prediction that had the shift late behind the tokens: the shift then lands some 6 to 8 us earlier (the tokens hold the queue for 8.5 us), the first Exp moves from 59.6 to about 52, and the time falls by 5 to 7 us, to 715. Rival: the tokens' later arrival delays the row scales of batch 1 by as much, and the time stays within 2 us of 721.5.

722.9, the rival's number, but not its cause. The first Exp came 4.6 us earlier, at 55.0, and batch 0 grew by 3.5. The row scales of batch 1 came no later: PE's wait for them at L325 was 1.8 us in both kernels and ended at 93.8 us, against 94.4. So the 4 us were lost ahead of it. What held the loop is the queue further on: the stores of the first chunks still stand behind the tokens. ScalarE may write the keys of the next chunk only when such a store has read its buffer, and PE may fill HIGH again only behind that write, so both stood:

```profile
67.19 0.67 ACT L915 ACTIVATE k<-ps,columns_sb 128x496 f32<-128x496 f32 x1 [8.45 <-DMA k_scratch<-k_parts]
```
```profile
68.48 2.07 PE L341 MATMUL ps<-w_centred,ctx_turned 128*124 128x256 f32 x4 [3.83 <-ACT k_parts L916]
```

**The combinations.** `best` joins mask late and later second; `best_shift` adds one exchange on SP's queue, `load_shift(1)` ahead of `load_turned(2)`; `best_batch0` adds the slots 28, 35, 42 in batch 0.

> The changed kernel with both changes that paid: the mask's reductions out of the way beside layer 1 (696.4 us alone) and the chunks of batches 2 and 3 at the slots 6, 11, 18, 25 (709.5 alone). Theory A, the two act in different batches and add up: 721.5 - 25.1 - 12.0 = 684.4 us (682 to 689), 3.5 to 4% below the kernel before. Rival B, the later last chunk runs into batch 3, where POOL's queue now also holds the mask loads: batch 3 keeps 4 us or more, 689 or above.

682.6: the two add up.

> The same as the kernel with both changes, and the shift of batch 1 is sent before the load of the context of batch 2 (0.8 MB) on SP's queue in place of behind it. By the prediction's step (that load ahead of the shift costs 2 us, 11.7 to 14.5 in the trace) PE's wait for the shift falls from about 14 to 11 us and the time by 2 to 3 us. Rival: the wait is for something else (the stores of the last chunk, 11.7 us of it were there before), and the time stays within 1 us.

680.0, as expected. PE's wait for the shift of batch 1, in the kernel after and here (13.9 us in `best`):

```profile
181.39 0.69 PE L389 MATMUL ps<-bias_g,bias_w 64*124 64x512 bf16 x2 [14.45 <-DMA q_side<-shift]
```
```profile
178.17 0.68 PE L389 MATMUL ps<-bias_g,bias_w 64*124 64x512 bf16 x2 [11.24 <-DMA q_side<-shift]
```

> The fastest kernel so far (680.0 us), with the last three chunks made in batch 0 (those of batch 1) at the slots 28, 35, 42 in place of 26, 33, 40. Theory A, also here the second chunk comes too soon after the first (PE waits 5.3 us for table products in batch 0): 3 us or more less, 677. Rival B, no softmax finish lies between them in batch 0, so nothing is gained, and the sample of batch 1 at slot 45 meets the last chunk: the same or up to 4 us more.

678.6, 1.4 us less and between the two; by the ratios it is 5 us less, so how much the slots give is open. PE's waits at L389 for Exps fell from 8.6 to 5.4 us. It is the fastest version, 4.8% below the kernel before.

## Why the prediction was wrong

- **The failed step is "The mask beside layer 1: +3 (0 to +12)".** It measured 27.7 us (no mask). The step priced 16 reductions of 0.97 us, which cost nothing (reductions only). It did not ask when the loads land. There is one buffer, and POOL issues a load only after the piece before is reduced. In 5 of the 16 places DVE came to the reduction before the load had landed, 18.9 us in all, and in batches 3, 5 and 6 the gate or the choice of experts stood behind it. About half of the cost is PE's waits there, the rest its lower clock behind them, which no term had. The step's upper bound of 12 had no row for a load behind it. With 27.7 in place of 3 the forecast would have been 716.7.
- **The loop of layer 0: its terms add to -0.1 us (-9, +9.6, 0, +2, -2.7), and it measured +16.5.** This is the second part that failed; the next points take its terms one by one. Without the mask the kernel took 693.8 us, inside the range. That is luck in part: the start gained 7 us more than its term, and layer 0 lost 13 in that profile where the terms had nothing.
- **The mask leaving layer 0: put at nothing.** The kernel before with the mask moved got 8.3 us back in batches 0 and 1 of its one profile. That term was missing, and in the other direction.
- **LOW is held longer: +9.6.** As a wait it was sized right. The trace of after has 5.3 us of it in batch 0 and 9.8 in batches 1 and 2, 3.3 and 3.4 at the two second chunks where the step had 4.2; before it was 4.5 in batches 1 and 2, so the waits grew by 10.6. What it left out is the clock behind such a wait: moving the second chunk gave 15 us for 5.7 us of waits, and one piece gave 14 to 16 us where the whole term was 9.6.
- **PE's work in the loop: -9 (its own terms add to -9.4).** Batch 2 at a clock of 1.00 takes PE 77.09 us before and 74.18 in later second, -2.9 where the step has about -3.6. In the changed kernel the lower clock hid it: 78.38.
- **ACT's new work: 0.** PE waited 11.5 us for Exps at L389 in layer 0, 0.3 before. This is ScalarE's line, the rival that ended slower, at a fraction of the size that it needed to decide. How much of the 11.5 is ScalarE's waiting for POOL was not separated, since later parts only moved those waits; short parts gives 5 to 7 us for the length of the writes, where the term was 0.
- **The start: -22.7.** It was -29.7. The first 38 us moved 203 GB/s, where it was 177 before; the first keys were placed from 26.4 us on where the step had 41, and the tokens of batch 1 took 8.5 us on the queue and not 12, so they were issued by 51.4 where it had 65.5. Half of these 14 us were lost again: the shift, issued at 51.5, let the first scores start at 58.5, and the step had no time for the shift behind the tokens. That the shift is late behind the tokens was right, that it matters was not: shift first moved the first Exp and not the end.
- **Hand-overs.** The row scales of batch 1 took 1.8 + 5.8 us against 11.0 before: -3.4 where 0 was put, inside its bounds. The shift of batch 1 took 14.5 against 11.7 [rows 6]: +2.8 for the +2, and the exchange on SP's queue shows that it was the load of the context. Of the 10.8 us in three waits of [rows 10] one of 1.8 is left: the other two, 5.9 us, are gone where -2.7 was said (the fall from 4.9 to 1.8 is in the -3.4 already).
- **The pieces.** No overlap was the rival, with 0.22, and it is right. Its own price, 0.45 us a chunk, is right as well (0.42 measured); it decided nothing.

In batch 0 PE's waits grew from 23.5 to 33.3 us, which is more than the stage's +8.7. Of layer 0's 16.5 us a later second chunk gives 12 to 15 back (with its clock) and single pieces give 14 to 16; the two must overlap, since both shorten the same wait, but they were not run together. How ScalarE's share divides between occupation and order was not settled.

## What to carry to other kernels

Price a moved check by when its data lands and by what stands behind it in the in-order engine that consumes it, not by its busy time; with a single buffer each load can start only when the piece before is reduced. Put such work where the engine next waits anyway: the same 16 loads and reductions cost 27.7 us in one order and 2.6, not told from nothing, in another. And do not price a wait of PE by its length alone. Here the clock behind it added nothing to a wait of 2.13 us (before, batch 2), nearly the length again to one of 3.28, more than the length to one of 3.71 (batch 5: PE busy 60.5 us for 55.9 without the mask), and 3.2 us to one of 7.78 (batch 3: 64.4 for 61.1).

## What the runs showed of the hardware

- Four DVE instructions of 32 x 496 that read PSUM start 0.64 us apart on the same partitions, and 0.74 to 0.76 when each reads and writes another group of 32. A product of 32 partitions takes as long as one of 128, 0.73 us.
- PE's granted clock was 1.00 ahead of a wait of 3.3 us and 0.55 in the 6.2 us behind it. Behind the wait of 3.71 us in batch 5 it was 0.50 for 13 us. Of what later second gave back in batches 1 and 2, 9.4 us were PE's busy time and 5.7 its waits.
- A mask load of 400 KB took 3.4 or 4.5 us from issue to landing (medians of the pieces of 801 and of 800 columns), but 10.8 us in batch 3, where 2.4 MB of keys, 0.9 MB of values and the expert weights had been issued on SP's queue just ahead, and 10.2 and 10.1 us in batches 5 and 6. That the loads on SP's queue are what slowed it was not tested. The window of the wait in batch 3 (columns as in [rows 2]) has the DMA engines 91% busy:

```profile
371.00:382.00 11.00, 3.22 (x33) 1.61 (x31) 2.80 (x6) 3.27 (x5) 0.56 (x1) 0.83 0.91 255
```
